# Attention sum of a graph network: five gather slots become four, gathers are written out, and additions stand ahead of one-hots

## The reference, cut to what matters

```python
for every edge e, head h:
    score[e, h] = clip(sum(q[dst[e], h] * k[src[e], h]), -10, 10)
    weight[e, h] = exp(score[e, h])
sum_v[n, h] = sum of weight[e, h] * v[src[e], h] over the edges e with dst[e] == n
sum_w[n, h] = sum of weight[e, h] over the same edges
y[n, h] = sum_v[n, h] / sum_w[n, h]          # a node with no edge gets 0
```

## Time and profile before

| | us |
|---|---|
| median of 3 runs (3507.44 to 3513.9) | 3513.81 |
| the profiled execution, its own time | 3502.91 |
| its span, from the first to the last instruction | 3501.1 |
| DVE's first to last turn in this stage (start of the L1987 copies) | 1543.3 to 2203.2 |

### The profile page before, as it was taken

How to read it: one execution, slowest core, us unless ns; L and a number is a source line. 1 busy time by engine, 2 the same in 40 slices (tenths; PEclk the granted TensorE clock), 3 DMA queues, 4 the chain that set the end, 5 groups by cost and what they waited for, 6 DMA issues and landing times. The chain is left out here.

```text
span 3501.1 us, 64268 instructions
## 1 busy us (share of the span) xinstructions
PE 2533.4 (72%) x17097; PEld 2041.1 (58%) x17098; DVE 2164.9 (62%) x4323; ACT 1280.5 (37%) x2474; POOL 1305.4 (37%) x1010
## 2 busy tenths in 40 slices
PE   5547555877589999657777777579664535999997
PEld 5425344666467777445555555468454424889976
DVE  7655455544478888557777777565346866544445
ACT  1432213211345554322222222253467734444541
POOL 0068785788100000057888888600000101111125
PEclk9668755988689999779999999779777755999998
DMA  5238683333000000167777777200000003466633
GB/s 139 82 87 222 165 211 79 78 84 82 17 28 9 18 18 9 53 166 185 192 191 189 191 193 190 68 24 0 16 1 0 0 0 129 149 225 238 231 125 87
DMA packets 248205, 365.03 MB, mean 104 GB/s; under 512 B 119043, under 2 KB 174688, under 8 KB 243740
## 3 DMA queue, kind: packets, MB, share of 16 engines
q0 software_dynamic: 154752, 174.53, 20.5%
q1 hardware_dynamic: 80476, 177.02, 15.7%
q10 hardware_dynamic: 12864, 12.06, 1.2%
HBM read 314.80 MB, written 47.76 MB: 104 GB/s over the span
## 5 line engine op out<-in xcount | busy, mean ns | idle before, releaser
L916 POOL DMA_INDIRECT ms_got<-gather,edge_src x400 | 522.4, 1306 | 167.3 <-issue 117.1
L1840 POOL DMA_INDIRECT as_gkv<-gather_kv,as_index x340 | 463.8, 1364 | 108.6 <-issue 100.3
L964 PE MATMUL ms_total<-ms_got,ms_hot 125*125 125x256 f16 x1040 | 182.6, 344 | 168.0 <-DVE ms_hot L937 138.3
L1957 PE MATMUL as_total<-as_gkv,as_hot 125*125 125x264 f32 x850 | 223.5, 413 | 77.0 <-DVE as_summed L817 70.1
L964 PEld LDWEIGHTS ms_total<-ms_got,ms_hot 125*125 x1040 | 157.3, 177 | 200.5 <-issue 199.7
L1630 ACT ACTIVATE ex_h<-ex_up,ex_now 128x313 f32<-128x313 f32 (+1 forms) x320 | 195.8, 612 | 197.0 <-PE ex_up L695 189.8
L1957 PEld LDWEIGHTS as_total<-as_gkv,as_hot 125*125 125x125 f32 x850 | 160.6, 197 | 118.6 <-issue 91.4
L1832 POOL IOTA as_node<- 125x25 f32 x1 | 0.2, 156 | 605.0 <-POOLq L120 605.0
L2954 DVE CAST moe_hidden<-moe_h 128x256 f16<-128x256 f32 (+1 forms) x336 | 101.6, 302 | 199.6 <-ACT moe_h L2891 199.6
L2891 ACT ACTIVATE moe_h<-moe_up,wring 128x256 f32<-128x256 f32 (+1 forms) x336 | 163.2, 486 | 127.5 <-PE moe_up L695 82.6
L1932 PE MATMUL as_picked<-y_rows,as_pick 125*125 x1060 | 150.9, 292 | 47.1 <-issue 45.7
(11 more groups left out here) (503 smaller groups left out, 5964.0 us busy)
## 6 DMA issues: line engine op xcount, KB each, us to landing
wring<-wsplit SPq DMA_DIRECT2D x33, 2052.0 KB
as_dsts<-in_dst SPq DMA_DIRECT2D x83, 305.2 KB
wsplit<-mix_split SPq DMA_DIRECT2D x32, 512.0 KB, 5.0
mix_raw<-in_L_ffn_W1p SPq DMA_DIRECT2D x16, 512.0 KB, 7.6
mix_raw<-in_L_ffn_W2p SPq DMA_DIRECT2D x16, 512.0 KB, 10.0
results<-moe_made SPq DMA_DIRECT2D x32, 256.0 KB, 7.5
ms_got<-gather,edge_src POOLq DMA_INDIRECT x400, 4.2
gather_kv<-qkv_out SPq DMA_DIRECT2D x5, 1120.0 KB
```

The source lines that it names most:

```text
L916: pool.indirect_dma_start(out=self.got[:, s, j, :], out_offset=None, in_=self.m.gather0, in_offset=bass.IndirectOffsetOnAxis(ap=self.m.edg ...
L964: ins = pe.matmul(self.total[:, visit % 2, 0:C], self.hot[:, visit % RING, j, :], self.got[:, s, j, p * C:(p + 1) * C], start=(j + p == 0) ...
L1840: pool.indirect_dma_start(out=gkv[s][:, j, 0:2 * C], out_offset=None, in_=m.gather_kv, in_offset=bass.IndirectOffsetOnAxis(ap=index[:, s, ...
L1957: ins = pe.matmul(total[:, visit % RING, 0:W], hot[:, s, j, :], gkv[s][:, j, C:C + W], start=(j == 0), stop=(j == J - 1))
```

## The change

Inside `attention_sum` only:

- four gather slots in place of five, all in buffers of their own; `qk`, `apart` and `none` get buffers of their own too
- the copies of row numbers are gone: POOL takes them from `m.edge_src` directly, with its gathers written out one after another, and waits on a new semaphore `s_free`, which DVE raises when it begins the visits of a group
- POOL gathers 81 groups, not 84
- two banks of `total` in place of four, three buffers of `pick` in place of four, two buffers of `hot` in place of five
- in a visit, DVE's addition stands ahead of its one-hot, and PE waits for that addition
- the loops of DVE, PE and ACT have 16 groups in a turn (DVE and PE had 5, ACT 10); SP's loads and the last 25 multiplications are written out

The core of the diff:

```diff
-        PICKS = 4
-        SLOTS = 5
-        index = ph.sb("index", [R, SLOTS, J], I32)
+        PERIOD = G // CHUNKS
+        GATHERED = 4
+        PICKS = 3
+        LATE = 2
...
-        total = ph.ps("total", [R, RING, 512])
+        total = ph.ps("total", [R, LATE, 512])
...
-                def gather(s):
+                for g in range(G + 1):
+                    s = g % GATHERED
+                    if g >= GATHERED:
+                        pool.wait_ge(s_free, g - GATHERED + 2)
+                        pool.sem_inc(s_pace, 1)
                     for j in range(J):
                         pool.indirect_dma_start(
                             out=gkv[s][:, j, 0:2 * C], out_offset=None, in_=m.gather_kv,
-                            in_offset=bass.IndirectOffsetOnAxis(ap=index[:, s, j:j + 1], axis=0)
+                            in_offset=bass.IndirectOffsetOnAxis(ap=m.edge_src[:, g, j:j + 1], axis=0)
                         ).then_inc(s_got[s], 16)
-
-                for s in range(SLOTS - 1):
-                    pool.wait_ge(s_index, s + 1)
-                    gather(s)
-                with pool.Fori(0, G // SLOTS) as i:
-                    for s in range(SLOTS):
-                        pool.wait_ge(s_index, i * SLOTS + (s + SLOTS))
-                        pool.sem_inc(s_pace, 1)
-                        gather((s - 1) % SLOTS)
...
+                def sums(n, s, bounds):
+                    first, count, before = bounds
+                    pe.wait_ge(s_spread, n + 1)
+                    pe.sem_inc(s_pace, 1)
+                    with pe.Fori(0, count) as k:
+                        visit = pe.snap(before + k)
+                        pe.wait_ge(s_hot, visit + 1)
+                        pe.wait_ge(s_added, visit + (1 + LATE))
+                        pe.sem_inc(s_pace, 1)
+                        for j in range(J):
+                            ins = pe.matmul(total[:, visit % LATE, 0:W], hot[:, s % 2, j, :],
+                                            gkv[s][:, j, C:C + W], start=(j == 0), stop=(j == J - 1))
+                        ins.then_inc(s_total, 1)
...
-                def next_index(g, s):
-
-                    nxt = m.edge_src[:, bass.ds(g, 1), :].rearrange("p a j -> p (a j)")
-                    dve.tensor_copy(index[:, s, :], nxt).then_inc(s_index, 1)
...
+                def visits(n, s, bounds):
+                    first, count, before = bounds
+                    dve.wait_ge(s_total, before + LATE)
+                    dve.sem_inc(s_pace, 1)
+                    dve.sem_inc(s_free, 1)
+                    with dve.Fori(0, count) as k:
+                        visit = dve.snap(before + k)
+                        tile = dve.snap(nc.s_assert_within(first + k, 0, T - 1))
+                        dve.wait_ge(s_total, visit + LATE)
+                        dve.sem_inc(s_pace, 1)
+                        adder.add(visit, tile)
+                        dve.scalar_tensor_tensor(out=hot[:, s % 2, :, :], in0=repeat_mid(m.row_no[0:R, :], J),
+                                                 scalar=node[:, bass.ds(tile, 1)],
+                                                 in1=repeat_last(m.edge_dst[:, n, :], R),
+                                                 op0=ALU.add, op1=ALU.is_equal).then_inc(s_hot, 1)
...
-                with dve.Fori(0, G // SLOTS) as i:
-                    v.enter(i, SLOTS)
-                    for s in range(SLOTS):
-                        n = i * SLOTS + s
-                        first, count, before = group_bounds(dve, m, n)
-                        scores(n + 1, i + (s + 1) // SLOTS, (s + 1) % SLOTS)
-                        dve.wait_ge(s_total, before + LAG)
-                        dve.sem_inc(s_pace, 1)
-                        next_index(n + SLOTS - 1, (s - 1) % SLOTS)
+                with dve.Fori(0, CHUNKS) as c:
+                    v.enter(c, PERIOD)
+                    for s in range(PERIOD):
+                        n = c * PERIOD + s
+                        bounds = group_bounds(dve, m, n)
+                        scores(n + 1, c * (PERIOD // GATHERED) + (s + 1) // GATHERED, (s + 1) % GATHERED)
+                        visits(n, s, bounds)
+                        weigh(n + 1, (s + 1) % GATHERED)
...
-                for s in range(SLOTS):
-                    dve.wait_ge(s_got[s], (G // SLOTS + (1 if s < SLOTS - 1 else 0)) * (16 * J))
+                for s in range(GATHERED):
+                    dve.wait_ge(s_got[s], 16 * J * len(range(s, G + 1, GATHERED)))
```

More of the change, by code:

```diff
@@ L1793, in attention_sum @@
     with phase(nc, "as") as ph:
-        PICKS = 4
-        SLOTS = 5
-        index = ph.sb("index", [R, SLOTS, J], I32)
+        PERIOD = G // CHUNKS
+        GATHERED = 4
+        PICKS = 3
+        LATE = 2
         W = C + X8
[L1798 to L1802, removed]
+        summed = ph.sb("summed", [R, T, W])
+        gkv = ph.sb("gkv", [R, GATHERED, J, C + W])
+        gkv = [gkv[:, s, :, :] for s in range(GATHERED)]
+        pick = ph.sb("pick", [R, PICKS, J * R], F16)
         q16 = m.q16
@@ L1807, in attention_sum @@
         node = ph.sb("node", [R, T])
[L1809 to L1810 removed]
+        apart = ph.sb("apart", [R, J * R], BF16)
         zeros = ph.sb("zeros", [R, R], F16)
         score = ph.sb("score", [R, J * X8])
[L1814 to L1817, removed]
+        qk = ph.sb("qk", [R, J * C])
+        hot = ph.sb("hot", [R, 2, J, R])
+        none = ph.sb("none", [R, T, X8])
         picked = ph.ps("picked", [R, 3, 512])
[L1819 to L1821 removed]
+        total = ph.ps("total", [R, LATE, 512])
+        s_node, s_zero, s_free = ph.sem("node"), ph.sem("zero"), ph.sem("free")
+        s_got = [ph.sem(f"got{s}") for s in range(GATHERED)]
         s_dst, s_dfree = [ph.sem(f"dst{s}") for s in range(2)], ph.sem("dfree")
@@ L1942, in _ @@
                 pick_q(1, group_bounds(pe, m, 1))
-                with pe.Fori(0, G // SLOTS) as i:
-                    for s in range(SLOTS):
-                        n = i * SLOTS + s
+                with pe.Fori(0, CHUNKS) as c:
+                    for s in range(PERIOD):
+                        n = c * PERIOD + s
                         ahead = group_bounds(pe, m, n + 2)
-                        first, count, before = group_bounds(pe, m, n)
+                        bounds = group_bounds(pe, m, n)
                         pick_q(n + 2, ahead)
-                        pe.wait_ge(s_spread, n + 1)
-                        pe.sem_inc(s_pace, 1)
-                        with pe.Fori(0, count) as k:
-                            visit = pe.snap(before + k)
-                            pe.wait_ge(s_hot, visit + 1)
-                            pe.wait_ge(s_added, visit + 1)
-                            pe.sem_inc(s_pace, 1)
-                            for j in range(J):
-                                ins = pe.matmul(total[:, visit % RING, 0:W], hot[:, s, j, :],
-                                                gkv[s][:, j, C:C + W], start=(j == 0), stop=(j == J - 1))
-                            ins.then_inc(s_total, 1)
+                        sums(n, s % GATHERED, bounds)
             @block.vector
@@ L2020, in _ @@
+                v.leave(CHUNKS)
+                first, count, before = group_bounds(dve, m, G - 1)
                 adder.finish(dve.snap(before + count), s_pace)
-                for s in range(SLOTS):
-                    dve.wait_ge(s_got[s], (G // SLOTS + (1 if s < SLOTS - 1 else 0)) * (16 * J))
+                for s in range(GATHERED):
+                    dve.wait_ge(s_got[s], 16 * J * len(range(s, G + 1, GATHERED)))
                 dve.wait_ge(s_picked, G + 2)
```

58 lines of the change are left out of this document (19 added, 39 removed).

## The result

| | before | after |
|---|---|---|
| median of four timed runs, us | 3511.81 (3507.44 to 3513.9) | 3684.74 (3676.1 to 3701.44) |
| ratio, 95% interval | 1 | 1.05 [1.0469, 1.0531] |
| profiled execution, us | 3502.91 | 3688.06 |
| 79 turns of DVE in the stage, us | 659.9 | 857.3 |
| mean of the 55 turns with one visit, us | 7.11 | 9.39 |

The kernel is 5% slower. The direction and the place were forecast, the size was not: 185 us on the profiled execution instead of 100.5, and 3685 instead of 3614, outside the range of 3555 to 3655.

The account below looks back on a forecast made before the run. No engine was full; DVE and POOL were taken as tied, five slots buffering between them. Lost slot +114.9 and end wait -14.4 gave +100.5 us on 3502.9, so 3603.4; 10.9 more for the median gave 3614, range 3555 to 3655.

Parts of the forecast that it names:

- The lost slot: Four gather slots for five: gathers start later, so the 79 turns take 774.8 us, 114.9 more than 659.9.
- Rivals 1 and 2: Gathers land sooner: fully, at best 3495 (0.06 with no-effect case); partly, landing 5.4, 3559 (0.18 with times up to forecast).
- the links: Chain over two turns: release to gather 0.9, a group's gathers 6.7, landing 7.4, scores 3.4, together 18.4 us.
- The signs: Expected profile: POOL waits for DVE some 100 us in about 77 pieces; DVE waits for rows in most turns.
- The end: Three groups fewer gathered: DVE's 14.67 us wait after its last addition goes, -14.4 us.
- In a second visit ... 11.2 stays: DVE's two-visit turns: addition ahead of one-hot adds 0.4 us, the dropped copy takes 0.37, so 11.2 us stays.
- the copy's 0.37: DVE's index copy, 0.17 us plus 0.2 idle ahead of it, saved in each turn once the copies go.
- Nearest are this stage's own returns ... so 0: Longer loop bodies on DVE and PE: four returns instead of 15, taken to cost 0.
- the upper bound of 26: Most the longer loop bodies were allowed to cost: four returns at 6.45 us, the longest written-out gather, 26 us.
- Rival 3: PE starves and its clock falls, lengthening two-visit turns: 3635 likelier, 3661 in full; chance 0.14, alone or with costly returns.
- 9.2: Forecast us for a one-visit turn of DVE: half of the 18.4 us chain from slot release to use.

## Why the prediction missed

**The lost slot: right, with some luck.** Its term of 114.9 us stands against 119.9: 779.8 us of turns in the run with four slots against 774.8. Rivals 1 and 2 (the landing gets much shorter) fell. The last gather's rows are used 7.7 us after its start in the timeline above. By the landings that the traces record, the median from the start of a group's last gather to the last landing of the group went from 7.9 to 6.4 us (5.2 to 10.0), while the DMA share went from 0.74 to 0.55. The Trainium skill's fit for such a transfer (DMA: Bandwidth & Descriptors, Anatomy of one DMA) gives an estimate of 2.6 us; the runs don't agree with it. The luck is in the links. In the changed kernel the landing is 1.0 us shorter in the median than the 7.4 taken, and the five gathers take 7.36 us where 6.7 was taken, since one of them lasts 2.5. In the run with four slots alone the landing is 6.0 in the median and 11.4 at the longest: many early ones and a few late ones came out near the 7.4 taken for all. The signs hold in part: POOL waits for DVE, but in 46 pieces and not about 77, and DVE waits for rows in 29 turns and not in most.

**The end: right.** The wait of 14.67 us has become 0.35 us ahead of the same operation, which starts at 2411.97.

**"In a second visit ... 11.2 stays": the step that failed.** The forecast charged the addition its own 0.42 us for 24 turns and took the copy's 0.37 back. Measured are 14.20 us. By the ratios the order and its banks cost 1.24% with four slots and short loops (about 43 us), 0.79% with four slots and long loops (28 us), 1.1% with five slots (38 us), and 0.68% in the kernel before (24 us). Each of the four is uncertain by 0.2 to 0.45%, so little can be read from their differences. No run changes the banks without the order; in the changed order PE starts on the one-hot (1.3 us after its start), which stands behind the addition, so that the two banks cost something of their own is unlikely, but not shown. Three things were missed.
- *The idle time ahead of an operation moves with it, and grew.* Ahead of the first operation of a turn there is idle time called "issue". With the one-hot first it is 0.9 us, with the addition first 1.33. With the 0.35 us to the one-hot behind it, a turn's first one-hot begins 1.86 us after the mark in place of 1.16. Before, the addition stood behind the one-hot, where the earlier trace rows show no idle time ahead of it. The idle time may be the work of DVE's sequencer on registers (the tile's address for `adder.add`). That is argued from the code, not shown.
- *The copy gave next to nothing back.* In the version with five slots and one-hots first, which has no copies, the one-hot begins 1.10 us after the mark, against 1.16 before, and not 0.37 sooner. A one-visit turn takes 6.72 us, against 6.82 in the earlier trace rows:

```profile
1738.84 0.18 DVE L1959 TENSOR_SCALAR as_score<-as_score 125x40 f32<-125x40 f32 x1
1739.94 0.92 DVE L1978 SCALAR_TENSOR_TENSOR as_hot<-row_no,as_node,edge_dst 125x625 f32<-125x625 f32 x1 [0.92 <-issue]
...
1745.56 0.18 DVE L1959 TENSOR_SCALAR as_score<-as_score 125x40 f32<-125x40 f32 x1
```

- *The second visit is a serial chain.* From one-hot to one-hot at the full clock it is 4.82 us with the addition first and 3.99 in the earlier trace rows. The addition itself is 0.35 of the 0.83; most of the rest is again time ahead of it, between the end of PE's sums and DVE's first operation (0.68 us in place of 0.29).

**"Nearest are this stage's own returns ... so 0": the second step that failed.** The long bodies cost 0.83%, some 29 us, give or take 13, about the upper bound of 26 which the working had. DVE's waits show 18.8 us of it directly. The timeline at the first return:

```profile
1713.49 1.48 DVE L1964 TENSOR_TENSOR as_gkv<-as_gkv 125x1280 f32<-125x1280 f32 x1
1720.11 1.49 DVE L1952 TENSOR_TENSOR as_qk<-as_picked,as_gkv 125x1280 f32<-125x1280 f32 x1 [5.13 <-issue]
```

This comes every 16 groups. The packets of the queue that loads instructions went with it (packets, MB, share), first the changed kernel:

```profile
q14 instruction: 100, 0.82, 0.1%
```

and with short loops:

```profile
q14 instruction: 55, 0.45, 0.0%
```

With 10 groups in a body it is 58. With only DVE's body long it is 78, and with only PE's and ACT's long 77. So those fetch too, and what they fetch costs nothing that shows. The Trainium skill has the rule that was weighed and set aside in the forecast (Runtime: NRT & Kernel Launch, Instruction fetch mechanics), that a taken branch out of the window stalls for a fetch; these runs agree, with about 5 us for each return on DVE. That a fetch is what DVE waits for is argued from the packets and the rule; no row names it. It was a mistake to take the lower bound because no row of before could show the cost. A body three times as long as the one in the trace is a case which that trace can't speak for.

**Rival 3, PE's clock: real, and beside the others.** It had a chance of 0.14, as another case beside the forecast, and its time was 3635 to 3661. The stage's clock fell from 0.93 to 0.79, and sums at the lower level are what a second visit waits for. With four slots alone it is at 0.90 and costs hardly anything (11.26 us for a two-visit turn). With additions first and four slots it is 0.80. The 24 second visits take 1.40 us more from one-hot to one-hot than the shortest, 34 us in all, and before it was 0.48, or 11 us. So an estimate of what the lower clock costs more than before is 22 us. It is part of what the ratios give to the order and to the loops: with short loops the clock is 0.80 with additions first and 0.88 with one-hots first.

**The sum again.** From the kernel before with four slots to the changed one the ratios go 3.43 (four slots), 2.93 (the rest of the change, with its order and its loops undone), 4.17 (the order put back), 5.00 (the long loops put back). The last two steps, +1.24 and +0.83, add up by construction, since each is the difference of two runs in a row. What is a test is that the first two agree once the surplus groups are counted, 3.15 and 2.93.

The turns give a second account. Those with two visits took 14.20 us and not 11.2, which is 72 us of the 82.5 by which all turns are over their forecast. Those with one visit took 9.39 and not 9.2, another 10. The 72 are, as estimates from the rows above: the order at the full clock 28 (0.70 + 0.83 ahead of the two one-hots, less the 0.35 of the addition that no longer stands behind, 24 times), the clock 22, and the four stops of the long bodies 19, which all fall in such turns. Together that is 69.

What stays open: with one-hots first the long loops cost 1.28% (1.0421 against 1.0293) and otherwise 0.83%, but the two differ by less than their uncertainties, so nothing more need be behind it. And no run changes the clock alone.

## What to carry to other kernels

A ring of buffers is priced by the chain from release to use, and that can be worked out from a trace in which the ring hardly ever binds. An operation that is moved can get idle time ahead of it that it did not have in its old place: price a turn from start to start, not by the operations' durations. Where an engine waits for PE's sums, it pays for PE's lower clock too. Where a loop body outgrows everything the trace holds, take the price of its return from the middle of the bounds, and keep a body as short as the rings allow.

## What the runs showed of the hardware

- Of the gathers in the middle of the stage of the changed kernel, 52 have only DVE's multiplication of the values by their weights (L1964) beside their first 1.21 us. Both of its inputs lie in SBUF. These gathers take 2.50 us in the median (2.11 to 2.54), as the one at 1591.12 in the timeline above. The 27 with only the multiplication of query and key beside them, one of whose inputs lies in PSUM, take 1.21, and so do the 116 with nothing beside them. It also matters when the two meet: 83 gathers that run into the addition and the one-hot in their later part (both inputs of the one-hot lie in SBUF) take 1.21 too. The Trainium skill (SBUF — State Buffer, Who interferes with whom) says that a DVE instruction with two inputs in SBUF contends with GpSimd's reads. The trace agrees.
- A loop body of 16 groups on DVE costs about 5 us at each return (18.8 us in 4), one of 10 groups nothing that shows.
- Landing times follow the load only a little: from the start of a group's last gather 6.4 us in the median at a DMA share of 0.55 against 7.9 at 0.74.
- Filler of no use to the result made the kernel faster (1.0346 against 1.0417) and raised the granted clock from 0.80 to 0.94. The gain lies ahead of the multiplication of query and key, not in the second visits that wait for PE; how it comes about is open.
